# Moving rows, coefficients and one average in the prologue of a two-layer convolution and attention kernel

## The reference, cut to what matters

```python
def _L0(x):                                   # x is normalised
    # a router picks 2 of 8 experts per image from mean and std of the channels
    shared = silu(group_norm(conv1x1_grouped(x, shared_w)))
    eo = grouped_conv3x3(x, fused_w)[topk_i]  # 2 chosen experts per image
    return shared + sum(silu(group_norm(eo)) * rw)
def _L1(x):                                   # x is normalised
    q, k, v = windows_8x8(qkv_w @ x + qkv_b)  # 8 heads of 16
    attn = softmax(q @ k.T / 4 + bias)
    return proj_w @ (attn @ v + depthwise7x7(v)) + proj_b
x = x + _L0(_gn(x)); x = x + _L1(_gn(x))
```

## Time and profile before

| | us |
|---|---|
| median of 3 runs | 713.45 |
| lowest, highest | 712.76, 716.25 |
| profiled execution, its own time | 711.36 |
| its span in the trace | 709.7 |
| TensorE matmuls busy | 589.7 (83%) |
| VectorE busy | 534.3 (75%) |
| ScalarE busy | 455.9 (64%) |
| GpSimd busy | 372.0 (52%) |

### The profile page before, as it was taken

One profiled execution on the slowest core, in us unless ns is written; L12 is line 12 of the kernel. 1 busy time (PEld: TensorE's weight loads), 2 busy tenths in 40 slices (PEclk: granted clock), 3 DMA queues, 4 the chain that ended last, 5 costly groups with the idle time before them and its releaser, 6 DMA issues.

```text
span 709.7 us, 19201 instructions
## 1 busy us (share of the span) xinstructions
PE 589.7 (83%) x6958; PEld 355.2 (50%) x6958; DVE 534.3 (75%) x967; ACT 455.9 (64%) x775; POOL 372.0 (52%) x599
## 2 busy tenths in 40 slices
PE   4417277889899898988999898989989898999892
PEld 3401032546465565645465565746556666544330
DVE  3962456788988989897888988898988878333791
ACT  2213456688787878878687877878787654455550
POOL 5146544777567767757567767766663201000372
PEclk9999577999999999999999999999999899999997
DMA  8832145647675756757474755667573254382393
GB/s 327 315 82 94 51 161 139 185 117 224 175 228 155 210 159 171 218 176 215 123 231 155 205 167 165 208 184 206 173 191 109 73 154 133 134 296 96 65 260 151
DMA packets 57603, 122.06 MB, mean 172 GB/s; under 512 B 12195, under 2 KB 29990, under 8 KB 57510
## 3 DMA queue, kind: packets, MB, share of 16 engines
q1 hardware_dynamic: 42982, 80.35, 36.7%
q0 software_dynamic: 13664, 37.35, 19.0%
q10 hardware_dynamic: 864, 3.15, 1.2%
HBM read 70.59 MB, written 41.81 MB: 158 GB/s over the span
## 4 chain that ended last, share of the span: by engine, by line
PE 43%; DVE 28%; issue 12%; POOL 6%; DMA 4%; ACT 3%; POOLq 2%; SPq 0%; DVEq 0%; ACTq 0%
PE g L1211 8%; PE pv L1276 5%; PE t L1261 4%; PE g L1191 4%; DVE mx L1004 4%; DVE vtmp L1050 4%; PE g L1294 4%; DMA vt<-x 4%; PE s L1250 3%; PE g L1221 3%; PE s L1316 3%; DVE st L990 3%; DVE xr L986 3%; DVE xr L981 3%; PE t L1316 2%
## 5 line engine op out<-in xcount | busy, mean ns | idle before, releaser
L649 ACT ACTIVATE y<-g 128x512 f32<-128x512 f32 x96 | 55.9, 600 | 86.1 <-PE g L1193 75.0
L1004 DVE TENSOR_REDUCE mx<-s 128x8 f32<-128x512 f32 x128 | 86.8, 678 | 25.4 <-PE s L1250 24.9
L1276 PE MATMUL pv<-vp,pt 128*64 128x34 f32 x2048 | 79.8, 222 | 16.0 <-DVE ot L1022 15.8
L1008 DVE TENSOR_TENSOR less<-s,mx 128x512 f32<-128x512 f32 x128 | 88.5, 691 | 4.4
L1261 PE MATMUL t<-ident,less 128*128 128x128 f32 x512 | 78.7, 277 | 7.2 <-ACT pt L721 7.2
L721 ACT ACTIVATE pt<-t 128x512 f32<-128x512 f32 x128 | 74.7, 595 | 13.3 <-PE t L1261 12.3
L958 DVE BATCH_NORM_STATS2 st<-y 128x6 f32<-128x512 f32 x96 | 63.2, 683 | 24.6 <-ACT y L649 23.3
L1276 PEld LDWEIGHTS pv<-vp,pt 128*64 128x64 f32 x2048 | 71.7, 140 | 18.9 <-issue 16.0
L1261 PEld LDWEIGHTS t<-ident,less 128*128 128x128 f32 x512 | 62.9, 145 | 33.9 <-issue 27.0
L1191 PE MATMUL g<-xa,wsa 128*128 128x512 f16 x192 | 58.0, 414 | 20.3 <-ACT y L649 13.3
L1211 PE MATMUL g<-xw,w 128*128 128x512 f32 x128 | 67.7, 654 | 1.0 <-DVE qhl L1033 1.0
(11 more groups left out here) (181 smaller groups left out, 1305.4 us busy)
## 6 DMA issues: line engine op xcount, KB each, us to landing
xs<-xhl POOLq DMA_DIRECT2D x16, 578.0 KB, 3.5
vt<-x SPq DMA_DIRECT2D x4, 2048.0 KB, 17.8
xin<-x POOLq DMA_DIRECT2D x16, 512.0 KB, 6.4
sq_d<-qhl SPq DMA_DIRECT2D x32, 256.0 KB, 2.2
sk_d<-khl SPq DMA_DIRECT2D x32, 256.0 KB, 3.0
stack<-sk_d SPq DMA_DIRECT2D x64, 128.0 KB, 3.7
stack<-sq_d SPq DMA_DIRECT2D x64, 128.0 KB, 3.9
vt<-vst SPq DMA_DIRECT2D x128, 64.0 KB, 3.1
```

The source lines that it names most:

```text
L649: act.activation(y[:, k, h * HALF:(h + 1) * HALF], g[at][:, :], ACT.Identity, scale=1.0 / (XSCALE * WSCALE)).then_inc(g_free[at], 1)
L1004: v.tensor_reduce(mx[:, p % 2, :], scored, AX.X, ALU.max).then_inc(sem["s_max"], 1)
L1008: v.tensor_tensor(less[:, p % 2, :].rearrange("p (h m) -> p h m", h=HEADS), scored, mx[:, p % 2, :].unsqueeze(2).to_broadcast([C, HEADS, T ...
L1276: last = mm(pvb[TOK * n:TOK * n + TOK, at:at + VC], pt[:, s % 3, i, n, :], vp[:, b % 2, 2 * p + n, i, :], start=True, stop=True)
```

## The change

GpSimd's prologue is put in another order at two places: `load_rows(1, 1)` and `load_x(2)` now stand before `x_affine(0)` and `choose_affine(1)`; `x_affine(1)` now stands before `choose_affine(2)` and `load_x(3)`. On TensorE `average(1, 0, 3, AV16)` moves from behind the k products of image 0 to between its q and k products, and on VectorE `group_means(1, 0)` moves likewise between the low parts of q and k. No instruction is added, removed or altered.

```diff
--- before.py
+++ after.py
@@ -571,19 +571,19 @@
             y_affine(0)
             load_rows(1, 0)
             load_weights(1, 1)
+            load_rows(1, 1)
+            load_x(2)
             x_affine(0)
-            load_rows(1, 1)
             choose_affine(1)
-            load_x(2)
             form_xn(2)
             save_xn(2)
             y_affine(1)
             for k in range(TOP):
                 load_weights(2, k)
                 load_rows(2, k)
+            x_affine(1)
             choose_affine(2)
             load_x(3)
-            x_affine(1)
             split_v(0)
             form_xn(3)
             images(step)
@@ -1101,10 +1101,11 @@
             y_stats(1, 0)
             y_stats(1, 1)
             y_stats(1, 2)
-            for n in range(2):
-                for h in range(2):
-                    low_qk(0, n, h)
+            for h in range(2):
+                low_qk(0, 0, h)
             group_means(1, 0)
+            for h in range(2):
+                low_qk(0, 1, h)
             for part in range(3):
                 residual(1, part)
             group_means(1, 1)
@@ -1363,10 +1364,11 @@
             average(0, 1, 1, AV4)
             convolve(1, 1)
             convolve(1, 2)
-            for n in range(2):
-                for h in range(2):
-                    project_qk(0, n, h)
+            for h in range(2):
+                project_qk(0, 0, h)
             average(1, 0, 3, AV16)
+            for h in range(2):
+                project_qk(0, 1, h)
             project_v(0)
             project_vt(0)
             convolve(2, 0)
```

## The result

| | before | after |
|---|---|---|
| median of the timed runs, first comparison | 713.11 us | 703.47 us (702.63 to 704.67, 4 runs) |
| ratio to before, 95% interval | | 0.9858 [0.9826, 0.989] |
| the same kernel once more, other chip time | 713.6 us | 704.39 us (6 runs), ratio 0.9874 [0.9834, 0.9913] |
| profiled execution, its own time | 711.36 us | 703.54 us |
| its span | 709.7 us | 701.8 us |

The time fell by about 9 to 10 us; the forecast was 705.8 us (713.45 less 7.7) in a range of 702.8 to 709.8. Both intervals of the ratio lie clear of 1.

What follows compares the result with a forecast made beforehand. The prediction took a prologue chain of waits ahead of the image loop as the bound. Terms 3.3 + 0.9 + 3.5 = 7.7 us off the 713.45 us median gave 705.8 us, range 702.8 to 709.8.

Steps and rivals of the forecast that it cites:

- the three gaps: Prologue waits: TensorE 3.31 us for rows, ScalarE 5.62 us for coefficients, VectorE 3.63 us for ScalarE.
- Part 1: GpSimd issues image 1's second rows before image 0's x coefficients; TensorE's 3.31 us row wait goes, coefficients 1.04 us later, hidden.
- rival 2: TensorE's clock rises before q once image 1's convolutions join: 1.7 us more, up to 3.4; 702.4 to 704.1 us; 12%.
- Part 2: Image 1's average between q and k: y means read 6.2 us sooner, silu 4.2 sooner, 0.9 from this move.
- The cover: Before k, TensorE's wait for VectorE's sums hides behind emptying half of q, 0.7 us later; cost taken as 0.
- Part 3: Image 1's x coefficients before expert choice and load of x 3: windowing at 109.0, 8.3 us sooner; 3.5 us counted.
- The split of the sum: Prologue gain divided as 3.3 (rows), 0.9 (average, at silu), 3.5 (coefficients, until VectorE binds): 7.7 us.
- What is late next: VectorE binds at the prologue's end: statistics and transpose back to back after scores, ending 115.27 instead of 123.02, 7.75 us sooner.
- TensorE's clock: Prologue: lower level in q (3.72 us), upper in k (1.98 us); the rise was assumed to move with q.
- the first burst had no effect: Argument against an earlier clock rise: TensorE's work from 80.3 to 84.67 us had not raised the level.
- Rivals 3 to 5: Gain partly given back, 707.6 or 709.3 us, 18%; no effect, 713 us, 7%; longer loop rhythm, 719 us, 3%.
- Rival 3: First loop step grows 1.9 us (707.6), or stacks, weights and rows land late (709.3 us); 18%.

Runs made afterwards that it cites:

- first profile: First profiled execution of the whole change; stretch, from VectorE's read of image 0's x means to its first v transpose's end, 34.1 us; ratio to before 0.9858.
- second profile before: The unchanged kernel profiled once more; stretch 41.9 us, q and k matmuls 1.98 us each.
- first profile before: The unchanged kernel's original profile; stretch 42.1 us, q matmuls 3.78 us, k 1.98; its own time 711.36 us.
- kernel with one fill: Whole change plus 14 unused matmuls in TensorE's gap between v products and image 2's first convolution; stretch 35.3 us, ratio to before 0.9898.
- second profile: The whole change, same code, profiled and timed again; stretch 37.0 us, q 2.74 and k 3.63 us; ratio to before 0.9874.
- kernel with four fills: Whole change plus unused matmuls in four TensorE gaps (42, 4, 14 and 4); stretch 31.7 us, ratio to before 0.9866.

## Why the prediction was right

**What bounds.** Right. In the profiles the gain came from the three gaps, ahead of the first transpose.

**Part 1.** The wait of 3.31 us went whole. The delay to the x coefficients, sized at 1.04 us, was 0.6, as the issues were quicker, and stayed hidden. The execution gave 1.05 us more, since the second of the joined convolutions ran at the upper level: rival 2, at 12%, is what happened in four of the six profiles that have part 1 and no fill, and this convolution ran at the upper level in none of the five without part 1. Its price was wrong in one term: q's 1.7 us count for nothing, because the average between q and k waits for the sums anyway (1.80 us in the first profile). Only the convolution's 1.05 us do. The second profile before shows the same: q at the upper level without part 1 is worth 0.2 us.

**Part 2.** The cover held: k 0.7 us behind the sums in every profile. The means of y were read 11.8 us behind the x means of image 0; the prediction had 13.1, and less the 1.05 of the level makes 12.1. Silu started straight behind the v copies.

**Part 3.** Right in place and about right in size: windowing at 27.1 us behind the read, where the prediction's 109.0 means 28.1, again the 1.0 of the level. From the x means to the windowing it is 2.2 us; the prediction had 1.75, because it took 10.4 us for image 2's issues, which took 10.8. The landing of x of image 3 was counted from the end of its issue; from the start, as for image 2, the sum gives 114.4 and not 115.0. Neither ScalarE nor GpSimd waited for it.

**The split of the sum.** Wrong, without effect on the total. "0.9 (average, at silu) + 3.5 (coefficients, until VectorE binds)" gives each part what was left over in one order. Alone, the average brings 2.6 us, because GpSimd's queue behind the y coefficients is the chain to the windowing whatever silu does. Part 3 brings 2.2 us on top of part 1; alone it shows that only between the x means and the windowing, and 0.6 us in its stretch.

**What is late next.** Named wrong. VectorE was not back to back: it stood 1.03 us for ScalarE's copy of image 2's second convolution, which TensorE did at the lower level (1.46 us at 109.16; 0.82 at 113.28 in the first profile before). The sum came out within 0.3 us (34.1 against 34.3) because two things outside it met: 1.0 us won by the level at image 1, and most of it lost again at image 2. That is luck. The kernel with one fill, whose first half went as the prediction assumed, took 35.3.

**TensorE's clock.** "I let the rise move with the q products" failed in the first profile, which is one of the prediction's own signs of being wrong, and held with one fill. The sentence "the first burst had no effect" was thin evidence: the same kernel does either. The second profile, which stayed low through both joined convolutions, shows that the moment is not the code's alone. So does an earlier burst of the same code: the three matmuls that began at 65.41 took 0.82 us in the second profile, those at 66.44 still 1.46 in the first, though the burst began at 59.78 in the one and at 60.65 in the other. The rule of the Trainium skill ("TensorE: Matmul & The Clock Gate", Part 1) that was weighed there, that activity releases the throttle, agrees with the first profile (1.46 us at 83.94, 0.82 at 85.76) and with the kernel with four fills (0.81 at 79.72).

**Rivals 3 to 5.** First step 29.30, steps of 31.2, no slower rhythm. A landing that takes the place of a wait was seen, though: the stacked q before the first scores, 0.65 us in the second profile and 1.70 with one fill. Rival 3 had named stacks, weights and rows together; in these executions TensorE waited for no other transfer inside the stretch.

**What stays open.** By the ratios the time fell by 9.0 and 10.1 us, the profiled stretch by 8.0 and 5.1. The lower ends of the intervals (7.8 and 6.2 us) allow 8.0 and not quite 5.1. From the first transpose on nothing speaks for a gain: 588.6 and 587.2 us in the two profiles before, 587.5 and 590.6 in the two after. The scatter sits mostly behind the loop: from the start of the last transpose of v to the end took 125.8 and 125.5 us in the two profiles before and 127.3 to 132.0 in the twelve others, while the fifteen steps from the first transpose to the last took 460.2 to 462.8 in all. Two executions of the kernel before are too few to say whether that end is longer after the change or these two were quick (both were faster than its median of 713 to 714 us). Most of the difference will be the scatter of single executions, but whether a part of the timed gain lies outside the stretch was not settled. What decides TensorE's level in one execution was not found either.

## What to carry to other kernels

In a prologue where no overlap fills the gaps, look on the engine with the in-order queue for an instruction that waits for a result, while issues behind it wait for nothing: moved ahead, they fill the wait, at the price of a later result that needs cover (here 0.6 us, hidden). Parts of such a change are worth what the chain leaves them, so a split of the sum depends on the order and should be tested by leaving parts out as well as by each part alone. And one profile of a stretch in which TensorE starts and stops is one draw: before a difference of 1 to 3 us is explained there, compare the matmuls' durations, level against level.

## What the runs showed that was not expected

The granted clock of a window did not always show the lower level. Windows of TensorE in the first profile after the change:

```profile
82.00:84.00 2.00, 2.00 (x6) 1.00 0.70 171
86.00:88.00 2.00, 1.98 (x8) 1.00 0.03 10
104.00:112.00 8.00, 7.93 (x33) 0.50 0.97 201
```

The clock column (behind the count in brackets) says 1.00 both at 82 and at 86 us, while three matmuls of the same shape took 1.44 us at 82.03 and 0.82 us at 86.83; only from 104 on does it say 0.50. In the first profile before, the column reads 0.50 from 80 to 96 us. Here the durations are the safer witness.

A step of 33.4 us stands at the same image in every profile (33.1 with four fills), before and after. GpSimd stands 3.6 us in front of one weight issue there (1.29 and 1.26 us in the step before it), in the kernel before at 320.45 and after at 313.73; no engine or transfer is named for it, and it was not looked into.

VectorE's last small sum of image 1 (L944, 128x3) took 2.01 us before and 1.91 after while GpSimd's subtraction over 1024 columns (L454) ran, against 0.16 for the same line at 122.98. In all fourteen profiles its end and that of the subtraction lie within 0.05 us of each other. The moved average waits 1.80 us for it, and k stands behind it too: with 0.16 us the sums would have been there 1.75 us earlier, by an estimate from these rows. No run moved the subtraction, so that it holds VectorE is read from these ends and not tested.
